# The values as TensorE's stationary operand, two groups at a time, in a cross-attention stage

## The reference, cut to what matters

```
q = ln_lat @ Wq;  k, v = split(concat([xn, ln_lat]) @ Wkv)     # 16 heads of 64
weight = einsum('bhld,bhnd->bhln', q * scale, k * scale)       # masked tokens: -max
weight = softmax(weight)                                       # over 4096 + 256 tokens
out = einsum('bhln,bhnd->bhld', weight, v) @ Wout
x = x + out
```

## Time and profile before

| | |
|---|---|
| runs, us | 1053.11, 1054.46, 1055.18 |
| profiled execution, own time | 1054.65 us |
| its span, first to last instruction | 1052.8 us |
| granted TensorE clock, mean | 0.995 |
| TensorE busy (matmul) | 1014.3 us, 96% |
| VectorE busy | 809.3 us, 77% |
| ScalarE busy | 666.8 us, 63% |
| GpSimd busy | 204.1 us, 19% |

### The profile page before, as it was taken

How to read it: one execution, slowest core, us unless ns; L and a number is a source line. 1 busy time by engine, 2 the same in 40 slices (tenths; PEclk the granted TensorE clock), 3 DMA queues, 4 the chain that set the end, 5 groups by cost and what they waited for, 6 DMA issues and landing times. The chain is left out here.

```text
span 1052.8 us, 25657 instructions
## 1 busy us (share of the span) xinstructions
PE 1014.3 (96%) x8683; PEld 943.1 (90%) x8684; DVE 809.3 (77%) x3001; ACT 666.8 (63%) x1550; POOL 204.1 (19%) x265
## 2 busy tenths in 40 slices
PE   6999999999999999999999998988999999999997
PEld 6899999999999999999999998977888999889887
DVE  7887777685877786787787777579879889889753
ACT  4765565674665665566565566478776876767753
POOL 0111111110111111111111111342015203263213
PEclk9999999999999999999999999999999999999999
DMA  6000000000000000000000100520010000110000
GB/s 208 18 13 2 10 1 1 12 12 4 12 2 0 12 13 3 13 2 0 12 13 2 35 2 2 166 38 2 1 41 21 2 1 21 35 48 2 1 22 21
DMA packets 28803, 21.64 MB, mean 21 GB/s; under 512 B 12094, under 2 KB 26267, under 8 KB 28699
## 3 DMA queue, kind: packets, MB, share of 16 engines
q1 hardware_dynamic: 28529, 20.21, 6.5%
q10 hardware_dynamic: 170, 0.07, 0.0%
HBM read 19.17 MB, written 1.05 MB: 19 GB/s over the span
## 5 line engine op out<-in xcount | busy, mean ns | idle before, releaser
L303 PEld LDWEIGHTS pv_ps<-v,pt 128*128 128x128 f32 x1792 | 214.9, 192 | 9.3 <-issue 2.8
L303 PE MATMUL pv_ps<-v,pt 128*128 128x65 f32 x1792 | 215.2, 272 | 3.2 <-DVE o L818 1.8
L796 DVE CUSTOM_DVE_ANT_0 s_sb<-s_ps,pen,mstate 128x256 f32<-128x256 f32 (+1 forms) x512 | 199.9, 446 | 13.9 <-issue 11.0
L510 ACT ACTIVATE probs<-s_sb,mbias 128x256 f32<-128x256 f32 (+1 forms) x512 | 203.2, 470 | 0.0
L670 POOL TENSOR_TENSOR o<-o,alpha 128x260 f32<-128x260 f32 x128 | 85.7, 669 | 561.3 <-ACT alpha L504 561.3
L519 ACT ACTIVATE pt<-turn 128x512 f32<-128x512 f32 x128 | 76.2, 595 | 123.0 <-PE turn L290 109.1
L290 PE MATMUL turn<-ident,probs 128*128 128x128 f32 x896 | 123.8, 278 | 0.1
L290 PEld LDWEIGHTS turn<-ident,probs 128*128 128x128 f32 x896 | 98.8, 145 | 9.5 <-issue 0.3
L818 DVE TENSOR_TENSOR o<-o,pv_ps 128x260 f32<-128x260 f32 x128 | 53.9, 421 | 46.1 <-PE pv_ps L303 34.7
L279 PE MATMUL s_ps<-kh,qh 64*128 64x256 f32 (+1 forms) x512 | 78.9, 304 | 2.9 <-DVE x L840 1.6
L768 DVE TENSOR_TENSOR kl<-proj,kh 128x512 fp32r<-128x512 f32 (+1 forms) x63 | 41.3, 655 | 51.5 <-ACT kh L497 51.0
(11 more groups left out here) (432 smaller groups left out, 2730.7 us busy)
## 6 DMA issues: line engine op xcount, KB each, us to landing
raw<-in_ctx SPq DMA_DIRECT2D x24, 128.0 KB, 2.0
f_wqkv_raw<-in_L_ffn_wqkv SPq DMA_DIRECT2D x6, 512.0 KB, 5.3
f_w_raw<-in_L_ffn_w SPq DMA_DIRECT2D x8, 256.0 KB, 5.1
f_w_raw<-in_L_ffn_w SPq DMA_DIRECT2D x2, 640.0 KB
wkv_raw<-in_L_xattn_Wkv SPq DMA_DIRECT2D x1, 1024.0 KB, 8.5
wout_raw<-in_L_xattn_Wout SPq DMA_DIRECT2D x1, 1024.0 KB, 12.5
f_wo_raw<-in_L_ffn_wo SPq DMA_DIRECT2D x2, 512.0 KB, 4.7
x<-in_x SPq DMA_DIRECT2D x1, 768.0 KB, 9.6
```

Of the source, the lines that this page charges most:

```text
L303: last = pe.matmul(t.pv_ps[:, u, :], t.pt[g % 2][:, u, kt, :], t.v[:, kt, h, :], start=(kt == 0), stop=(kt == kts - 1))
L510: last = act.activation(t.probs[g % 2][:, u, 0:kts * P], t.s_sb[g % 2][:, u, 0:kts * P], ACT.Exp, bias=t.mbias[:, at:at + 1], scale=0.125)
L796: last = dve.tensor_tensor_reduce(out=t.s_sb[g % 2][:, u, 0:width], in0=t.s_ps[g % 2][:, u, 0:width], in1=t.pen[:, 0:width], scale=1.0, sc ...
```

## The change

- **Weighted values** (`weighted_values`): the values of one head (128 keys by 64) are now stationary, in a half of the array's columns (head 0 of the group in columns 0 to 63, head 1 in 64 to 127), and the turned probabilities of both query tiles (256 columns) stream past. The output lies turned: (head, value column) on the 128 partitions by 256 query rows. It goes to a quarter of the even score buffer `s_ps[0]` (`output_bank`), for which TensorE waits until the even group's scores are read.
- **Two groups at odd steps** (`pair_at`): at odd j, groups j-4 and j-3, ahead of `turn_probs`.
- **Turning back**: ScalarE copies each group's output to SBUF (`store_outputs`, at the start of its odd step, behind the softmax of step j-1); TensorE turns both back (`turn_back`, behind `turn_probs`, ahead of the projection) into `pv_ps`, now 128 x 2 x 256; VectorE adds both groups behind its copy of the turned probabilities at odd j.
- **Sums**: each exponential writes its own sum through ScalarE's accumulator (`accum_out`), and GpSimd adds the four sums of a group to the 65th column of `o` in an instruction of its own behind the scaling. The ones column of `v` goes.
- Semaphore counts follow (`rescaled` counts two per group); two semaphores of the plan are merged with others; two small buffers of the plan lie in `onorm` now.

```diff
+            def pair_at(m, kind, prev, j):
+                return [now for now in (at_step(m, kind, prev, j - 4), at_step(m, kind, prev, j - 3)) if now] if j % 2 else []
+            def output_bank(g):
+                return t.s_ps[0][:, 2 - g % 2 * 2, :]
 # TensorE
-                for u in range(GU):
-                    h = 2 * g + u // QT
-                    for kt in range(kts):
-                        last = pe.matmul(t.pv_ps[:, u, :], t.pt[g % 2][:, u, kt, :], t.v[:, kt, h, :],
+                for kt in range(kts):
+                    for o, rows in enumerate((slice(0, DH), slice(DH, P))):
+                        last = pe.matmul(output_bank(g)[rows, :], t.v[:, kt, 2 * g + o, :], t.pt[g % 2][:, QT * o:QT * o + QT, kt, :],
                                          start=(kt == 0), stop=(kt == kts - 1))
+            def turn_back(pair):
+                for m, g, kts in pair:
+                    pe.wait_ge(s["ov_stored"], 8 * m + g + 1)
+                first_m, first_g, _ = pair[0]
+                if first_g or not isinstance(first_m, int):
+                    pe.wait_ge(s["o_added"], 8 * first_m + first_g)
+                for m, g, kts in pair:
+                    for qt in range(QT):
+                        last = pe.transpose(t.pv_ps[:, 1 - g % 2, qt * P:(qt + 1) * P], t.ov[g % 2][:, qt * P:(qt + 1) * P], t.ident[:])
+                last.then_inc(s["o_turned_back"], len(pair))
 # TensorE, body
+                    pair = pair_at(m, kind, prev, j)
+                    if pair:
...
+                        pe.wait_ge(s["s_read"], 8 * m + (j + 2 if kind else 2))
+                        for now in pair:
+                            weighted_values(*now)
                     now = at_step(m, kind, prev, j - 2)
                     if now:
                         turn_probs(*now)
+                    if pair:
+                        turn_back(pair)
...
-                    now = at_step(m, kind, prev, j - 3)
...
-                    if now:
-                        weighted_values(*now)
 # ScalarE
                     last = act.activation(t.probs[g % 2][:, u, 0:kts * P], t.s_sb[g % 2][:, u, 0:kts * P], ACT.Exp,
-                                          bias=t.mbias[:, at:at + 1], scale=0.125)
+                                          bias=t.mbias[:, at:at + 1], scale=0.125, accum_out=t.sums[:, at:at + 1])
+            def store_outputs(m, g, kts):
+                act.wait_ge(s["pv_done"], 8 * m + g + 1)
+                if g >= 2 or not isinstance(m, int):
+                    act.wait_ge(s["o_turned_back"], 8 * m + g - 1)
+                act.activation(t.ov[g % 2][:], output_bank(g), ACT.Copy).then_inc(s["ov_stored"], 1)
 # ScalarE, body, first in a step
+                    for now in pair_at(m, kind, prev, j):
+                        store_outputs(*now)
 # GpSimd
+                    pool.wait_ge(s["rescaled"], 16 * m + 2 * g + 1)
+                    pool.wait_ge(s["p_ready"], 8 * m + g + 1)
+                    pool.tensor_tensor(t.o[:, cols, DH], t.o[:, cols, DH], t.sums[:, cols], ALU.add).then_inc(s["rescaled"], 1)
 # VectorE, body
-                    now = at_step(m, kind, prev, j - 4)
-                    if now:
-                        add_output(*now)
...
+                    pair = pair_at(m, kind, prev, j)
+                    if pair:
+                        last_m, last_g, _ = pair[-1]
+                        dve.wait_ge(s["o_turned_back"], 8 * last_m + last_g + 1)
+                        for now in pair:
+                            add_output(*now)
```

More of the change, by code:

```diff
@@ L159, in value_part @@
     def value_part(u):
-        return t.v[:, u % 2, (u // 2) * NG:(u // 2 + 1) * NG, 0:DH]
+        return t.v[:, u % 2, (u // 2) * NG:(u // 2 + 1) * NG, :]
     def load_norm(eng, which):
@@ L386, in body @@
                         pe.wait_ge(s["q_ready"], 4)
+                    pair = pair_at(m, kind, prev, j)
+                    if pair:
+                        if prev is None and j == 3:
+                            pe.wait_ge(s["plan_rows"], 1)
+                        if kind is None and j == 3:
+                            pe.wait_ge(s["ot_lo"], 4 * b - 3)
+                        pe.wait_ge(s["s_read"], 8 * m + (j + 2 if kind else 2))
+                        for now in pair:
+                            weighted_values(*now)
                     now = at_step(m, kind, prev, j - 2)
@@ L465, in _ @@
             project_keys(0, KB)
-            pe.wait_ge(s["keys_spread"], 1)
-            pe.matmul(t.pv_ps[0:B, 1, 0:NCH + 1], t.row_of[:], t.listed[:], start=True, stop=True).then_inc(s["keys_listed"], 1)
+            pe.wait_ge(s["flags_ready"], 3)
+            pe.matmul(t.pv_ps[0:B, 1, 0:NCH + 1], t.row_of[:], t.listed[:], start=True, stop=True).then_inc(s["flags_ranked"], 1)
             pe.wait_ge(s["w_lo"], 3)
@@ L815, in add_output @@
                 cols = slice(GU * g, GU * (g + 1))
-                dve.wait_ge(s["pv_done"], 8 * m + g + 1)
-                dve.wait_ge(s["rescaled"], 8 * m + g + 1)
-                dve.tensor_tensor(t.o[:, cols, :], t.o[:, cols, :], t.pv_ps[:], ALU.add).then_inc(s["o_added"], 1)
+                dve.wait_ge(s["rescaled"], 16 * m + 2 * g + 1)
+                added = t.o[:, cols, 0:DH].rearrange("p (o q) d -> p o q d", q=QT)
+                dve.tensor_tensor(added, added, t.pv_ps[:, 1 - g % 2, :].rearrange("p (q o d) -> p o q d", q=QT, o=2), ALU.add
+                                  ).then_inc(s["o_added"], 1)
             def normalise_output(m, b, half):
@@ L822, in normalise_output @@
                 dve.wait_ge(s["o_added"], 8 * m - 4 + 4 * half)
+                dve.wait_ge(s["rescaled"], 16 * m - 8 + 8 * half)
                 dve.reciprocal(t.inv[:, cols], t.o[:, cols, DH]).then_inc(s["inverse"], 1)
@@ L851, in body @@
                 for j in range(NG if kind else 6):
-                    now = at_step(m, kind, prev, j - 4)
-                    if now:
-                        add_output(*now)
-                    if finish and j in (0, 3):
-                        normalise_output(m, b, j // 3)
+                    if finish and j == 0:
+                        normalise_output(m, b, 0)
                     if kind and j == 4 and not final:
@@ L863, in body @@
                         store_turned(*now)
+                    pair = pair_at(m, kind, prev, j)
[4 more added lines that the diff above has]
+                            add_output(*now)
+                    if finish and j == 3:
+                        normalise_output(m, b, 1)
                     if finish and j in (1, 2, 4, 5):
@@ L958, in plan_keys @@
                 dve.tensor_scalar(twice, t.iota[:], 2.0, None, ALU.mult)
-                dve.wait_ge(s["keys_listed"], 1)
+                dve.wait_ge(s["flags_ranked"], 2)
                 dve.tensor_copy(t.plan_rows[:, 0:NCH], t.pv_ps[0:B, 1, 0:NCH])
@@ L2562, in program @@
             t.kh, t.kl = (sb(n, [P, NG, KB], F32R) for n in ("kh", "kl"))
-            t.v = sb("v", [P, KT, H, DH + 1])
+            t.v = sb("v", [P, KT, H, DH])
+            t.ov = [sb(f"ov{k}", [P, L]) for k in range(2)]
             t.s_sb = [sb(f"s_sb{k}", [P, GU, KB]) for k in range(2)]
@@ L2566, in program @@
             t.pt = [sb(f"pt{k}", [P, GU, KT, P]) for k in range(2)]
-            t.mstate, t.mnew, t.mdiff, t.mbias, t.alpha, t.inv = (
-                sb(n, [P, H * QT]) for n in ("mstate", "mnew", "mdiff", "mbias", "alpha", "inv"))
+            t.mstate, t.mnew, t.mdiff, t.mbias, t.alpha, t.inv, t.sums = (
+                sb(n, [P, H * QT]) for n in ("mstate", "mnew", "mdiff", "mbias", "alpha", "inv", "sums"))
             t.o = sb("o", [P, H * QT, DH + 1])
             t.onorm = sb("onorm", [P, QT, H * DH])
+            t.key_row = t.onorm[:, 0, 0:P]
+            t.below = t.onorm[:, 1, 0:P].rearrange("p (b c) -> p b c", b=B)
             t.ot, t.ot_raw = split("ot", [P, 8, L])
```

21 lines of the change are left out of this document (8 added, 13 removed).

## The result

The changed kernel takes **1090.22 us** (median of 1089.03 to 1092.08) against 1054.76: ratio 1.0341, 95% interval 1.0322 to 1.0359. That is 35 us slower. Slower was forecast; 1057 was the point, so the size was far too small, inside the range of 1036 to 1100 but outside the 1046 to 1068 of the case thought likeliest. That the range holds it is luck: its upper part was there for column halves that run one after the other, and they do not. The span of its profiled execution is 1088.1 us.

A forecast was written before the change was run, and what follows sets the result against it. TensorE, busy all 39.56 us of a full-group item, was taken as the bound. Pair items -8, half items +10, latents items 0, opening item -1, tail +1: +2 on 1054.65, forecast 1057 us, range 1036 to 1100.

The forecast's parts named there:

- the case thought likeliest: Whole kernel: column halves overlap but TensorE waits for ScalarE's output copies; 1057 us, between 1046 and 1068, chance 0.57.
- Values on TensorE: Weighted values of two full groups: 16 passes in overlapping column halves take 2.1 us, or 3.6 without overlap.
- The new wait: Turning back waits 0.65 us for ScalarE's copies, beginning 3.57 us after T, the end of the even step's projection.
- Full groups: Two steps with full groups take 9.56 us against 9.80; 1.0 us gained per item, -8 us over 8 items.
- I looked for what is late next: Full groups: VectorE's second copy of turned probabilities loses its cover but just fits, costing nothing; ScalarE has a microsecond spare.
- Half groups: Half items: ScalarE's chain stays nearly as long while little work is removed; +2.9 us per item, +10 over four.
- Latents items: ScalarE's chain adds 2.4 us at step 4, steps 5 and 7 win 1.0 to 1.2 each; sum 0 for three.
- Opening item: The opening latents item, which finishes no batch, was to gain 1 us.
- the serial one: Rival: column halves run one after the other, values of two groups take 3.6 us; 1103 us, chance 0.2.
- TensorE sets the pace: Rival: ScalarE's copies come in time, two steps take 8.8 us; -42, 1012 us, halfway 1033; chance 0.13 wholly or partly.
- VectorE being late: Rival: VectorE's copy slips or its adds cost more, 0.5 us in 3 of 4 pairs; +18, 1075 us, chance 0.1.
- The rule on emptying PSUM: Skill's rule: tiling quickens TensorE but not the emptying of PSUM, so the gain is lost to ScalarE; no separate size.

The follow-up runs named there:

- both moves: Changed kernel with outputs turned back behind the projection (also step 3 of latents items) and results added ahead of the keys' lower part: 1050.70 us, ratio 0.9950.
- the projection ahead: Changed kernel, late turning back, results before keys; in pair and half items the odd step's projection precedes the probabilities' turning, value store earlier at steps 1, 3: 1050.18 us.
- the run that forces it: Changed kernel with both heads' values in the same half of the array's columns, so nothing runs side by side: 1148.05 us, ratio 1.0885.
- early penalties (projection behind): Changed kernel, late turning back, results and penalties before keys on VectorE, VectorE copying half groups' outputs, projection after the probabilities' turning: 1047.11 us, ratio 0.9928.

## Why the prediction came out as it did

- **Values on TensorE**: right. 2.1 us were forecast for two groups, 1.87 and some 0.1 of entry into halves were measured, and 3.60 without overlap against 3.6.
- **The new wait**: right in place and size, T+3.57 forecast and T+3.39 measured; 34 us in 47 places. Taking the accumulators out halves it (16.9), and moving the turning back leaves 12.8 in 14 places.
- **Full groups**: the pair of steps was right (9.56 forecast; 9.41 and 9.45 measured), but the item was not. "I looked for what is late next" went through VectorE's copy and stopped there. Step 3 has the token turning behind the value projection on TensorE, through the same bank, and it waits until ScalarE has stored the values. Before, the values of one group lay between the two. The row after:

```profile
330.34 0.65 PE L258 MATMUL proj<-ident,z 128*128 128x128 f32 x4 [0.76 <-ACT v L557]
```

0.69 to 0.82 us in each of 15 items, 11.6 us in all. In the 8 pair items it is 6 of the 7 us that were missed: steps 2 and 3 take 10.81 instead of 10.21. Beside it steps 0 and 1 gained nothing instead of 0.24, as TensorE waits 0.4 there for VectorE's maxima (the forecast had this as "just fits"), and steps 4 to 7 gained 0.1 more than forecast.

- **Half groups**: +11.3 against +11, in part by luck. A half item was to lose 2.9 us and lost 3.45: the token turning, which the forecast lacks, adds to it. The last one with the tail lost 1.0 instead of some 2, for a stretch at 1.2 GHz lies in that of the kernel before. For steps 2 and 3 the reason was wrong: no value waits for late probabilities; TensorE waits 0.98 for the copies and 0.82 for the value store. Steps 4 and 5 are as forecast, 6.67 us against 6.75: values, turn, a wait of 1.08 for the copy, and at once the next scores, with no projection to use the time:

```profile
371.01 1.08 PE L308 MATMUL s_ps<-pt,v 128*64 128x256 f32 x8
...
372.02 0.66 PE L298 MATMUL turn<-ident,probs 128*128 128x128 f32 x4
...
373.76 0.63 PE L321 MATMUL pv_ps<-ident,ov 128*128 128x128 f32 x4 [1.08 <-ACT ov L542]
...
374.31 0.33 PE L287 MATMUL s_ps<-kh,qh 64*128 64x128 f32 x2
```

- **Latents items**: the step that failed, "Sum 0". ScalarE's chain was right: +2.4 was forecast by step 4 and +3.2 measured over steps 0 to 3 of the second latents item, with 0.76 of token turning in it; steps 4 and 5 gained 1.1, as forecast. Steps 6 and 7 were to gain as much and lost 1.9. The count asked there whether the copies are in time, and not what the next scores wait for. They overwrite the bank from which VectorE adds the finished result; VectorE does so behind the lower part of the keys, which waits for ScalarE's store of the projection just made. On VectorE at that place, and then on TensorE:

```profile
437.74 0.69 DVE L802 TENSOR_TENSOR kl<-proj,kh 128x512 fp32r<-128x512 f32 x1 [3.98 <-ACT kh L520]
438.35 0.41 DVE L876 TENSOR_TENSOR x<-x,s_ps 128x256 f32 x1
```

```profile
439.12 0.39 PE L287 MATMUL s_ps<-kh,qh 64*128 64x256 f32 x2 [2.04 <-DVE x L876]
```

2.04 us, and 1.74 ahead of the scores of step 7, six times 1.9 on average; before, the values of one group stood there and 1.6 us in three places were left. Of the 15.7 us this makes 9.7 and the token turning 2.3. Another 3.2 are the clock. The same last step, from the scores of step 7 to those of the next item, in the first and the second latents item:

```profile
258.86:271.11 12.25, 10.21 (x78) 8.17 (x78) 4.78 (x18) 4.33 (x15) 0.82 (x2) 0.86 0.01 3
428.50:439.12 10.62, 8.58 (x77) 7.42 (x78) 4.78 (x18) 4.32 (x15) 0.82 (x2) 1.00 0.02 4
```

1.63 us more at a granted clock of 0.86, which is 3.4 of the 12.25 us at half speed; the third latents item has the same (12.20).

- **Opening item**: forecast -1, measured +2.5 with its begin. At its step 3 TensorE waits 2.50 us for the copies, since ScalarE splits the output weights ahead of them:

```profile
44.58 2.18 ACT L662 ACTIVATE wout_hi<-wout_raw 128x512 fp32r<-128x512 f32 x4
```

```profile
47.39 0.63 PE L321 MATMUL pv_ps<-ident,ov 128*128 128x128 f32 x4 [2.50 <-ACT ov L542]
```

Before, the same split stood there (L630, 2.18 us from 44.69) and TensorE waited for nothing behind it. Turning back late does not shorten the item (42.6): 1.1 us are then waited for the copies and 2.2 for VectorE ahead of the token turning. Of the versions that turn back late, it lasts 42.5 to 42.6 us in the five traces with a stretch at 1.2 GHz in it (so has the changed kernel's, 42.3) and 41.0 in the two without; here with both moves, and with the projection ahead, an edit that leaves this item alone (`prev is not None`):

```profile
19.95:62.50 42.55, 36.33 (x295) 29.71 (x294) 33.81 (x138) 33.65 (x104) 6.99 (x15) 0.96 0.06 15
```

```profile
19.71:60.73 41.02, 34.78 (x297) 28.29 (x296) 33.75 (x138) 33.69 (x104) 7.03 (x15) 1.00 0.06 18
```

- **Middle and latent stages**: forecast as untouched, and 6.3 us longer with the same instructions. Stretches from the last result of the cross stage to the first local scores, and from there to the end, before and then after:

```profile
669.50:715.30 45.80, 41.62 (x270) 36.22 (x270) 34.41 (x80) 31.63 (x70) 21.37 (x38) 1.00 0.42 118
715.30:1052.80 337.50, 319.60 (x2519) 290.33 (x2518) 263.51 (x781) 230.70 (x470) 94.95 (x94) 0.99 0.06 17
```

```profile
698.50:747.40 48.90, 42.99 (x270) 37.59 (x270) 36.66 (x80) 31.66 (x70) 21.38 (x38) 0.97 0.40 110
747.40:1088.10 340.70, 322.74 (x2519) 293.05 (x2518) 262.54 (x781) 230.66 (x470) 94.97 (x94) 0.98 0.06 17
```

TensorE's busy time rises by 1.4 and 3.1 us for the same 270 and 2519 matmuls, while the granted clock (before the last two numbers) is 0.97 and 0.98 instead of 1.00 and 0.99. With the cross stage, the changed kernel's trace has 27.3 us at 1.2 GHz, that of before 10.2. At 1.5 us for each 3.4 this is an estimated 7 to 8 of the 35 us. The forecast has no term for it.

Of the rivals, the serial one is refuted by the run that forces it. "TensorE sets the pace" did not happen in the changed kernel, but is what the late turning back gives in steps 6 and 7 of pair items: 8.85 us. (Its terms add up to 44 us, not 42.) VectorE being late was minor (5.3 us) until the other waits were out, and was then the next bound.

The rule on emptying PSUM from the Trainium skill ("TensorEngine Tiling (Array Packing)", section "PSUM Bottleneck") agrees with the trace as far as full steps go: the halves saved TensorE 1.7 us in two steps, and the copy behind ScalarE's softmax kept 0.7 of it, turning back 0.4. But the limit is the place in the queue and not the emptying itself: the two copies take 0.63 us, and no pair item waits for them once their reader stands behind the projection. The larger part of the loss is not of that kind.

## What to carry to other kernels

When a block of work is taken out of an in-order queue or moved within it, list every wait that stood behind it, to the end of the loop and into the next iteration: each was covered by that block and now shows with its own length. Put the consumer of a slow copy behind work that needs nothing from it; that one move gave 23 of the 35 us back, at a lower clock than it had before. Only when such waits are out does a faster matmul form pay, here 1.3%. And before a step of a few microseconds is credited to an edit, look at the granted clock on both sides, and at the part of the trace that the edit can touch.

## What the runs showed of the hardware

Column halves of the array do run beside each other for FP32 products, which appear as two matmul instructions (passes) each: 16 passes of 256 columns in 1.87 us, 0.117 each, against 0.225 in one half.

Reading out ScalarE's accumulator behind an exponential of 256 columns holds the engine 0.09 us more: they begin 0.49 us apart, where the earlier trace rows give 0.40 without it.

The mean granted clock differs between executions of one kernel, and the time follows it. The changed order with early penalties (projection behind) took 1042.5 us in an execution with 0.997 and 1051 to 1053 us in those with 0.985; the changed kernel without accumulators 1065 us at 0.995 and 1072 to 1074 us at 0.987 to 0.989. The executions of the kernel before lay between 0.992 and 0.997, those of the changed kernel between 0.987 and 0.992. Over the 137 executions on record, each taken against the mean of its own kernel, 0.001 of mean granted clock goes with 0.66 us. In the traces the loss sits in short stretches at the lower level of 1.2 GHz. They lie in every stage: 10.2 of the changed kernel's 27.3 us in the cross stage, and 23.9 of 44.4 us with the turning back late alone. An item of the cross stage lasts 1.5 to 1.6 us longer with 3.4 us of it inside (opening item 42.55 against 41.02, half item 38.40 against 36.89, last step of a latents item 12.25 against 10.62). In the middle and latent stages, which no edit touches, it is worth 4.5 us of TensorE's busy time for the same matmuls (1.4 + 3.1), of the 6.3 us by which they are longer. Why TensorE falls to the lower level more often with the changed cross stage stays open.
